# Routing layer 0 unit by unit inside its attention mixing, with one sorted buffer for both layers

## The reference

```python
xn = layernorm(x)
# layer 0, feed-forward: 4-head attention over the 8 sequences at one position, then top-1 experts
y = layer_norm(xn + mha(xn, Wqkv, bqkv, Wo, bo), g1, be1)
idx = argmax(y @ Wg.T, axis=-1)                       # one of E = 8 experts
for e in range(8):
    m = (idx == e)[:, None]
    out = out + m * (relu(y @ W1[e] + b1[e]) @ W2[e] + b2[e])    # 128 -> 512 -> 128
z = layer_norm(y + out, g2, be2)
x = x + attention0(xn) + z                            # 16 heads, amplitudes and phases
xn = layernorm(x)
# layer 1: each token goes to its two best experts, silu(xe @ w1) * (xe @ w3) @ w2
x = x + attention1(xn) + moe1(xn)
```

## Time and profile before

| | us |
|---|---|
| median of three runs | 1260.5 (1257.8 to 1261.35) |
| profiled execution, whole | 1268.18 |
| its span | 1266.6 |
| mixing, 14.9 to 160.9 | 146.0 |
| middle 0, 160.9 to 374.6 | 213.7 |
| attention 0, 374.6 to 671.9 | 297.3 |
| middle 1, 671.9 to 806.3 | 134.4 |
| experts 1, 806.3 to 985.0 | 178.7 |
| attention 1, 985.0 to 1266.6 | 281.6 |

### The profile page before, as it was taken

The page is one execution under the profiler, slowest core; times in us unless marked ns, Lnnn a source line. Parts: engine busy times, 40 slices in busy tenths (PEclk is TensorE's granted clock), DMA queues, the critical chain, the costliest instruction groups (busy, mean ns, idle before and its releaser), DMA issues. The chain is left out here.

```text
span 1266.6 us, 25796 instructions
## 1 busy us (share of the span) xinstructions
PE 990.7 (78%) x8908; PEld 644.5 (51%) x8908; DVE 811.0 (64%) x1771; ACT 694.8 (55%) x1325; POOL 579.8 (46%) x833
## 2 busy tenths in 40 slices
PE   2789654989858988888864563399999599999997
PEld 1456432777654544444422342288888244554453
DVE  1566341767649999999924776033333799999992
ACT  1356443868614777777753643122222377777775
POOL 3467546111022466655650566311110467777774
PEclk9899876999986999999985665699999599999998
DMA  4321032678752222222201443466664111121110
GB/s 134 108 51 51 35 109 83 177 199 232 214 162 71 70 73 77 75 72 70 66 18 52 121 121 104 137 181 195 183 193 141 44 43 53 53 55 51 53 49 27
DMA packets 151763, 126.71 MB, mean 100 GB/s; under 512 B 23760, under 2 KB 134272, under 8 KB 151648
## 3 DMA queue, kind: packets, MB, share of 16 engines
q1 hardware_dynamic: 141904, 107.05, 29.7%
q0 software_dynamic: 8016, 17.71, 4.8%
q10 hardware_dynamic: 1728, 0.46, 0.2%
HBM read 77.83 MB, written 44.70 MB: 97 GB/s over the span
## 5 line engine op out<-in xcount | busy, mean ns | idle before, releaser
L2098 ACT ACTIVATE attend_probs<-attend_attend_ps 128x512 f32<-128x512 f32 x640 | 354.2, 600 | 156.4 <-PE attend_attend_ps L2172 145.8
L2172 PE MATMUL attend_attend_ps<-attend_q,attend_ks 50*128 50x512 f16 (+3 forms) x1024 | 236.8, 308 | 23.2 <-ACT attend_probs L2098 20.6
L2061 POOL TENSOR_SCALAR_AFFINE_SELECT attend_probs<-attend_probs 128x512 f32<-128x512 f32 x256 | 159.6, 638 | 158.6 <-ACT attend_probs L2098 157.5
L2140 PE MATMUL attend_attend_ps<-attend_ks,attend_q 48*128 48x512 f16 (+3 forms) x1024 | 191.2, 317 | 25.5 <-DMA attend_ks<-k_stack 16.3
L2185 PE MATMUL attend_attend_ps<-attend_probs,attend_vals 128*32 128x512 f32 (+3 forms) x2048 | 183.4, 455 | 0.0
L2267 DVE TENSOR_REDUCE attend_neg_max<-attend_attend_ps 128x2 f32<-128x1024 f32 x128 | 155.5, 1215 | 13.9 <-PE attend_attend_ps L2152 13.2
L2152 PE MATMUL attend_attend_ps<-identb,stairs 64*128 64x128 bf16 (+1 forms) x1280 | 144.1, 213 | 0.0
L2172 PEld LDWEIGHTS attend_attend_ps<-attend_q,attend_ks 50*128 50x128 f16 x1024 | 70.4, 94 | 122.7 <-ACT attend_probs L2098 68.4
L2269 DVE TENSOR_REDUCE attend_neg_max<-attend_attend_ps 128x2 f32<-128x768 f32 x128 | 121.5, 949 | 7.2 <-PE attend_attend_ps L2152 6.9
L2152 PEld LDWEIGHTS attend_attend_ps<-identb,stairs 64*128 64x128 bf16 x1280 | 103.6, 100 | 19.8 <-issue 4.7
L1845 PE MATMUL experts_experts_ps<-experts_rowsT,experts_w_in 128*128 128x256 f32 (+1 forms) x468 | 110.9, 387 | 1.6 <-ACT experts_rowsT L1794 1.5
(11 more groups left out here) (319 smaller groups left out, 1939.0 us busy)
## 6 DMA issues: line engine op xcount, KB each, us to landing
experts_w_in<-in_L_ffn_w_dram SPq DMA_DIRECT2D x78, 176.0 KB, 2.4
q_stack<-middle_parts SPq DMA_DIRECT2D x24, 256.0 KB, 3.4
k_stack<-middle_parts SPq DMA_DIRECT2D x24, 256.0 KB, 3.6
attend_q<-q_stack SPq DMA_DIRECT2D x64, 96.0 KB
attend_ks<-k_stack SPq DMA_DIRECT2D x64, 96.0 KB
middle_w_in<-in_L_ffn_W_dram SPq DMA_DIRECT2D x23, 256.0 KB
middle_w_out<-in_L_ffn_W_dram SPq DMA_DIRECT2D x23, 256.0 KB
experts_rows<-sorted POOLq DMA_DIRECT2D x39, 128.0 KB, 2.5
```

What stands on the lines that cost most here:

```text
L2061: pool.affine_select(out=block_, in_=block_, compare_op=ALU.is_ge, fill=0.0, base=0, pattern=[[0, GH], [1, P]], channel_multiplier=-1).the ...
L2098: act.activation(probs[:, u.par, 2 * c + side, :], ps[:, PROB + side, :], ACT.Exp, scale=SCALE ** -2)\
L2140: pe.matmul(ps[:, bank + side, col:col + (qt + 1) * P], q[rows(side, KR), g, pair, qt * P:(qt + 1) * P], ks[rows(side, KR), g, pair, 0:(qt ...
L2172: mm = pe.matmul(ps[:, PROB + side, col:col + S - kt * P], ks[rows(side, KM), g, pair, kt * P:(kt + 1) * P], q[rows(side, KM), g, pair, kt ...
```

## The change

In layer 0 the routing moves into `mix0`, unit by unit, and each expert gets a place of PLACE rows in a buffer `k.sorted` that both layers use (144 tiles of 256 rows). So the row of a token needs only the counts of the tokens before it. VectorE picks the expert of unit t-6 in step t, TensorE forms the ranks of a unit ahead of the next unit's logits, VectorE turns them into rows behind it. GpSimd writes y to `k.y` itself, and scatters units 0 to 2 at the end of its steps 7 to 9. ScalarE writes zeros over the whole buffer, in 18 DMAs of 8 tiles, three in each of steps 1 to 6; the zeros are set in `setup`. The first scatter waits for all of them.

In `middle0` only the last unit is routed, the tables of the tiles follow, and GpSimd scatters units 3 to 7 as its first work. It waits for tables and scatters and then loads the rows of the tiles itself, for the first four at once and later for tile n+3, ahead of its sine product. `turn_rows` waits only for the rows; `into_hidden` waits for the weights. The tiles begin in step 2. At the end VectorE works out where the results lie (`result_rows`, as in layer 1), for the attention's gathers. `middle1` no longer stores zeros.

```diff
@@ mix0, GpSimd
-                if u.past(2):
-                    pool.wait_ge(y_turned.sem, y_turned.done(u - 2))
-                    pool.wait_ge(y_kept[u.par].sem, (u - 2).n // 2 * 16 + 16)
-                pool.tensor_tensor(y[:, u.par, :, :], res_g[:, :, :], wide(k.row[:, R_BE1, :]), ALU.add)\
+                pool.tensor_tensor(k.y[:, u.n * QT:(u.n + 1) * QT, :], res_g[:, :, :], wide(k.row[:, R_BE1, :]), ALU.add)\
                     .then_inc(y_ready.sem, 1)
...
+                if 0 <= t.n - 7 < SCATTERED:
+                    pool.wait_ge(y_ready.sem, y_ready.done(t - 7))
+                    scatter_unit(pool, k, (t - 7).n)
@@ mix0, ScalarE
+            act.wait_ge(k.zero_set.sem, 1)
             for t in steps:
+                if 1 <= t.n <= 6:
+                    for n in range((t.n - 1) * FILLS // 6, t.n * FILLS // 6):
+                        act.dma_start(k.sorted[n * FILL * ROWS:(n + 1) * FILL * ROWS, :].rearrange("(a p r) d -> p a (r d)", a=FILL, p=P),
+                                      k.zeros[:, :].unsqueeze(1).broadcast_to([P, FILL, ROWS * D // P])).then_inc(k.zero_out.sem, 16)
@@ mix0, TensorE and VectorE
+                if u.past(1):
+                    route_ranks(pe, k, u.n - 1, ps[:, PT, QT * E:2 * QT * E])
                 for j in range(QT):
                     mm = pe.matmul(ps[:, PT, j * E:(j + 1) * E], yT[:, columns(j)], k.gateT[:, 0, :], start=True, stop=True)
...
+                if active(t, 6, UNITS):
+                    route_choice(dve, then, k, (t - 6).n)
...
+                    if u.past(1):
+                        then(route_row_of(dve, k, u.n - 1, ps[:, PT, QT * E:2 * QT * E]))
                     dve.tensor_copy(k.logits[:, u.n * QT:(u.n + 1) * QT, :],
...
+                    if u.past(1):
+                        route_rows(dve, then, k, u.n - 1)
@@ new functions
+def route_choice(dve, then, k, n):
+    logits, hot, ties = k.logits[:, n * QT:(n + 1) * QT, :], k.hot[:, n * QT:(n + 1) * QT, :], k.ties[:, :, :]
+    then(dve.tensor_reduce(k.best[:, :], logits, X_AXIS, ALU.max))
+    then(dve.tensor_tensor(ties, logits, k.best[:, :].unsqueeze(2).broadcast_to([P, QT, E]), ALU.is_equal))
+    then(dve.tensor_tensor(ties, ties, k.weight[:, :].unsqueeze(1).broadcast_to([P, QT, E]), ALU.mult))
+    then(dve.tensor_reduce(k.best[:, :], ties, X_AXIS, ALU.max))
+    then(dve.tensor_tensor(hot, ties, k.best[:, :].unsqueeze(2).broadcast_to([P, QT, E]), ALU.is_equal))
+    for j in range(QT):
+        following = k.ahead[:, n % 2, j + 1, :] if j < QT - 1 else k.ahead[:, (n + 1) % 2, 0, :]
+        ins = dve.tensor_tensor(following, k.ahead[:, n % 2, j, :], hot[:, j, :], ALU.add)
...
+def route_ranks(pe, k, n, rank):
+    pe.wait_ge(k.hot_done.sem, k.hot_done.done(n))
+    pe.matmul(rank, k.before[:, :], k.hot[:, n * QT:(n + 1) * QT, :].rearrange("p j e -> p (j e)"), start=True, stop=False)
+    return pe.matmul(rank, k.ones[:, :], k.ahead[:, n % 2, :, :].rearrange("p j e -> p (j e)"), start=False, stop=True)
...
+def scatter_unit(pool, k, n):
+    pool.wait_ge(k.rows_ready.sem, k.rows_ready.done(n))
+    if n == 0:
+        pool.wait_ge(k.zero_out.sem, 16 * FILLS)
+    for t in range(n * QT, (n + 1) * QT):
         done = k.scattered[0][t % 4]
         if t >= 4:
             pool.wait_ge(done.sem, t // 4 * 16)
-        pool.indirect_dma_start(k.sorted0, bass.IndirectOffsetOnAxis(ap=k.rank_row[:, t:t + 1], axis=0), k.y[:, t, :], None)\
+        pool.indirect_dma_start(k.sorted, bass.IndirectOffsetOnAxis(ap=k.rank_row[:, t:t + 1], axis=0), k.y[:, t, :], None)\
@@ middle1, SP
-            for e in range(E):
-                row = sp.value_load(k.tail_row[0:1, e:e + 1], min_val=e * PLACE, max_val=e * PLACE + T)
-                sp.dma_start(k.sorted1[bass.ds(row, ROWS), :].rearrange("(a p) d -> p a d", p=P), zeros[:, :, :])\
-                  .then_inc(tail_out.sem, 16)
-            sp.wait_ge(tail_out.sem, tail_out.done(0))
@@ middle0
-    FIRST_TILE = 3 * PARTS_OF_STEP
+    FIRST_TILE = 2 * PARTS_OF_STEP
@@ middle0, GpSimd
-            pool.wait_ge(routing.rows_ready.sem, 1)
-            scatter(pool, k)
-            for u in range(B):
+            def load_rows(n):
+                if n >= RING:
+                    pool.wait_ge(turned.sem, turned.done(n - RING))
+                row = pool.value_load(k.tile_row[0:1, n:n + 1], min_val=0, max_val=E * PLACE + (SPARE - 1) * ROWS)
+                pool.dma_start(rows[:, n % RING, :, :], k.sorted[bass.ds(row, ROWS), :].rearrange("(a p) d -> p a d", p=P))\
+                    .then_inc(rows_in[n % RING].sem, 16)
...
+            for n in range(SCATTERED, B):
+                scatter_unit(pool, k, n)
+            pool.wait_ge(tables_ready.sem, 1)
             for done in k.scattered[0]:
                 pool.wait_ge(done.sem, NT // 4 * 16)
+            for n in range(RING):
+                load_rows(n)
+            for t, part, n in order:
+                if n >= 1 and tile(n + 3):
+                    load_rows(n + 3)
+                if part == 2 and row(t - 2):
+                    sine_products(t - 2)
@@ middle0, TensorE
             def turn_rows(n):
-                pe.wait_ge(loaded[n % RING].sem, (n // RING + 1) * (LOADS * 16))
+                pe.wait_ge(rows_in[n % RING].sem, (n // RING + 1) * 16)
...
             def into_hidden(n):
                 pe.wait_ge(rowsT_ready.sem, rowsT_ready.done(n))
+                pe.wait_ge(loaded[n % RING].sem, (n // RING + 1) * (LOADS * 16))
```

263 lines of the change are left out of this document (106 added, 157 removed).

## The result

The changed kernel takes 1252.0 us, median of 4 runs (1248.5 to 1252.1), against 1260.3 us for the kernel before in the same comparison (1257.8 to 1261.4). The ratio is 0.993, 95% interval 0.9908 to 0.9953. Timed again it was 0.9931 (0.9917 to 0.9945). That is a gain of 8.3 to 8.6 us where 19.2 were forecast. The time lies in the forecast's range of 1229 to 1256, near its upper end, and about 11 us of the forecast gain are missing.

The account below looks back on a forecast made before the run. No engine is full in the mixing, and the start of the tiles sets middle 0's end. Terms 8.0 - 25.3 + 9.6 - 7.0 - 4.5 = -19.2 us against the median of 1260.5 gave 1241.3 us, range 1229 to 1256.

Parts of the forecast that it names:

- Middle 0: First expert phase, 213.7 us before: start -25.3, tile steps +9.6 and the wait for rows -7.0 us.
- The start: Middle 0: with twenty scatters left, TensorE turns the first rows at about 192.5 against 217.75, -25.3 us.
- The relief: Middle 0: GpSimd asks for rows three tiles ahead, removing TensorE's waits for rows; -7.0 us (0 to -10).
- the rival of no relief: Middle 0: waits for rows stay, through bandwidth or late weights, so the sum is -12.2 us, 1248 us; 15%.
- The extra step: Middle 0: tiles starting a step earlier add one full step (+20.3) and save 10.7 at the end; +9.6 us (7 to 13).
- Mixing, zeros: Mixing: ScalarE's 18 fills, 18.9 MB, just fit its waiting but meet loads and stores; +1.5 us (0 to 4).
- The rival in which fills hold ScalarE: Mixing: each DMA issue waits until the one ahead is drained, +28 us, 1269 us; 8%.
- Mixing, GpSimd: Mixing: four scatters exceed GpSimd's 2.59 us of waiting by 2.5 us, in two steps; +4.9 us (2.5 to 7.5).
- The rival of slower scatters: Mixing: scatters beside VectorE take 1.78 us instead of 0.96, +17 us at most instead of +4.9; 1250 us, 10%.
- Mixing, routing: Mixing: choices cost nothing in steady state; ranks and rows around the last logits add 1.0 and 0.6, together +1.6 us.
- Middle 1: End of middle 1: SP's eight tail stores go, then the scatters' landing ends the phase; -4.5 us (-2 to -6).
- VectorE's hole: Middle 0: VectorE's unexplained standstill of 22.39 us returns, delaying the tiles' steps by about 10 us; 1251 us, 7%.

Follow-up runs that it names:

- first9: Changed kernel with the tiles beginning in step 3, as before the change, instead of step 2; ratio to the kernel before 0.9858.
- fills_2to7: Changed kernel with each group of three fills one step later, in steps 2 to 7, still ahead of ScalarE's normalisation; 1246.0 us, ratio to the kernel before 0.9887.
- fills2: Changed kernel with only step 1's three fills moved behind ScalarE's first normalisation; ratio to the kernel before 0.9944.
- scattered0: Changed kernel with no unit scattered in the mixing, all 32 scatters at the start of middle 0; 1264.4 us, ratio to the kernel before 1.0027.
- pairs: Changed kernel with the mixing's twelve scatters two a step over steps 7 to 12 instead of four over 7 to 9; ratio to the kernel before 0.9899.
- routing_late: Changed kernel with no scatter and no routing in the mixing, all of it at the start of middle 0; ratio to the kernel before 1.0125.

## Why the forecast was wrong

- **Middle 0, right in sum, and partly by luck.** Forecast -22.7 us, measured -22.3 and -21.9. The start: 33.2 us to the first expert matmul, as worked out. The relief: real, and the rival of no relief fell, but it is 10 to 11 us by first9 and not 7. The extra step: forecast +9.6 (7 to 13), and it costs 14 us, since the last unit's products and stores end the phase alone. The two errors cancel (-25.5 - 10.7 + 13.9 = -22.3). That first9 gains 9.5 us as a whole is not the forecast's 9.6: it is 14 less the 4.5 us of later start. The forecast paid for this step and didn't see that it need not be paid: more than half of unit 2's row work goes into TensorE's wait of 10.7 us for the first rows.
- **Mixing, zeros: the step that failed.** The forecast had +1.5 us. It took the fills' instant from SP's, which stood behind two units' loads at 23.38, and looked at ScalarE's idle time. On ScalarE nothing stands ahead of step 1's fills, so they leave at 15.45 and meet the one load that everything waits for. Measured +6.2 us at the first normalisation and +5.4 at the eighth; fills_2to7 shows 0.9 without that collision. The rows it used for ScalarE's cover are of steps 2 and 7; step 1 wasn't looked at. It also took the DMA engines as a quarter busy, which is the mean of the phase; in the stretch of the fills (15.5 to 90 us) they were at 0.36 before and are at 0.78 now. The rival in which fills hold ScalarE fell where it was placed: three issues take 2.5 us (forecast 1.6) ahead of the normalisation, and ScalarE's wait behind them still shows 1.5 us or more in each step. It does come up when two groups are close: in fills2 the second takes 7.82 us to issue.
- **Mixing, GpSimd.** Overrun forecast at 2.5 us in two steps, 4.9 in all. Seen in the steps: the sixth y starts 5.0 to 5.9 us later than with two a step. At the end it is 1.5 to 3.0 us by the profiles of scattered0 and pairs, and 2.6 to 4.8 us by their times. The mechanism is right; whether the term is too large stays open. The rival of slower scatters fell: all but the first of each four take 0.96 us.
- **Mixing, routing.** Forecast +1.6 us; routing_late shows some 2.4. What was missed is TensorE's wait for VectorE's choice ahead of the last two logits (3.30 and 0.79 us). The choice stands behind the statistics of a later unit in VectorE's order.
- **Sum of the mixing.** With 2.5 us for the scatters it is 5.4 + 2.5 + 2.4 = 10.3 us of the 11.4 to 14.6 measured. The rest lies in the drained end, where two executions of the same kernel differ by 3 us; it is not attributed. Of the 11 us that are missing in the gain, the zeros are the largest part that a run shows: 4 to 5 us over their term, and fills_2to7 gets 5.5 us back.
- **Middle 1.** Forecast -4.5 us since the tail stores ended the phase. They didn't. In after the last scatter ends 7.4 us before the next phase, and in before it was 7.5 (798.79 to 806.26) and 8.4 in the second profile:

```profile
785.35 0.97 POOL L1162 DMA_INDIRECT sorted<-middle_scaled,rank_row  x1 [0.30 <-issue]
793.76 0.23 DVE L1790 TENSOR_SCALAR experts_half_bias<-row 128x128 f32<-128x128 f32 x1 [14.77 <-PEq L194]
```

  The phase is 131.2 us against 134.4 and 132.6 in the two profiles of before, so -1.4 to -3.2; where that comes from stays open.
- **VectorE's hole** of 22.39 us didn't come back; TensorE waits 2.89 us at that place. What it was stays open.

With the measured phases the sum is 14.6 - 22.3 - 3.2 = -10.9 us from the first two profiles and 12.5 - 21.9 - 1.4 = -10.8 from the second two. The medians say -8.3 and -8.6. The profiled execution of after is the fastest of its four (1248.5 against a median of 1252.0), and that is more than the 2.4 us between the two accounts. Left out of these sums is attention 0, 1.6 and 2.4 us shorter in the profiles of after. In most kernels with the same change it is back at 297 to 298 us, so that is those executions and not the change.
- **Slips in the working.** The spread that waits 3.92 us stands in the earlier trace rows, not in the earlier trace rows. The rival of the fills that hold ScalarE counts 3 us in two steps and names three; it would be 31 us. Neither bears on the forecast.

## What to carry to other kernels

A DMA that is moved to another engine leaves when that engine's order lets it, and at a phase's start that can be at once: read what stands ahead of it there, and which load the first work waits for. The same 18.9 MB cost 0.9 us here in a place where each load beside them had a whole step to land, and 5.4 to 9.4 us in the four others, where an awaited load stood beside them, stores stood behind them in the queue, or their issues held a copy that another engine needed. And when a wait is shortened, ask which neighbouring work now fits into what is left of it: here starting the tiles as early as possible was worth less than filling the wait. And before phases are compared, a second profile of the unchanged kernel shows which differences are only those of one execution.

## What the hardware showed unexpectedly

Some of VectorE's small operations get longer beside GpSimd's 128x512 elementwise work, by much more than their own length. In after, VectorE and GpSimd:

```profile
138.75 1.58 DVE L800 TENSOR_TENSOR mix_score<-mix_score,mix_sums 128x128 f32<-128x128 f32 x1
...
141.69 0.89 DVE L879 TENSOR_TENSOR ties<-logits,best 128x32 f32<-128x32 f32 x1
...
168.39 1.04 DVE L905 CAST rank_row<-row_f 128x4 uint32<-128x4 f32 x1
```

```profile
138.89 1.28 POOL L519 TENSOR_TENSOR mix_res_g<-mix_res_n,row 128x512 f32<-128x512 f32 x1
...
141.47 2.07 POOL L532 TENSOR_TENSOR mix_probs<-mix_score,mix_same 128x512 f32<-128x512 f32 x2
...
168.14 1.26 POOL L522 TENSOR_TENSOR y_all<-mix_res_g,row 128x512 f32<-128x512 f32 x1
```

A 128x128 product took 1.58 us where it takes 0.29 in the undisturbed steps, a 128x32 comparison 0.89 where it takes 0.19, a 128x4 cast 1.04 where it takes 0.17. Each ends within 0.2 us of the end of the GpSimd operation beside it: the product at 140.33 (140.17), the comparison at 142.58 (the first of the two spreads ends at about 142.5), the cast at 169.43 (169.40). Reductions and copies out of PSUM in the same places kept their length (L904 and L848, 0.17 to 0.19 us). So did a comparison with two inputs beside a 128x4 operation of GpSimd (0.19 us from 163.97, inside GpSimd's 1.02 us from 163.75). The Trainium skill, "Trainium Architecture — The Big Picture", section "What this means for kernel authors", says that VectorE and GpSimd share a pair of ports to SBUF as an exclusive lock. The rows agree with that, as the slowed operations end with GpSimd's, though no run here separates it from other causes.

The other number is the queue behind large fills. Three fills of 1 MB take 0.40, 0.60 and 1.55 us to issue on ScalarE, the third already slowed, and eight stores of 32 KB behind three fills on SP take 9.5 us to issue instead of 3.6.

```profile
77.31 0.40 ACTq L571 DMA_DIRECT2D sorted<-zeros  x1
...
77.73 0.60 ACTq L571 DMA_DIRECT2D sorted<-zeros  x1
...
78.36 1.55 ACTq L571 DMA_DIRECT2D sorted<-zeros  x1
```
